# Values of two sets in succession, four buffers of probabilities, and weight rounding in two groups, in a causal attention stage

## The reference

```python
x = x + attn(layernorm(x))            # x: (4, 1024, 256); 16 heads of 16, causal
    q, k, v = proj(x)                 # 256x256 weights and a bias each
    scores = einsum('bhqd,bhkd->bhqk', q, k) / 4 ; future keys masked
    out = softmax(scores) @ v ; out @ wo + bo
x = x + ffn(layernorm(x))             # depth 2: local attention (8 heads of 64, window 128),
                                      # then a gated feed-forward, 256 -> 2*682 -> 256
```

## Time and profile before

| | us |
|---|---|
| median of three runs (2153.69 to 2154.58) | 2154.39 |
| the profiled execution | 2154.2 |
| its span | 2152.4 |
| one group of the causal stage without weight rounding | 31.89 |
| the two groups with it | 39.20 and 40.22 |

### The profile page before, as it was taken

How to read it: one execution, slowest core, us unless ns; L and a number is a source line. 1 busy time by engine, 2 the same in 40 slices (tenths; PEclk the granted TensorE clock), 3 DMA queues, 4 the chain that set the end, 5 groups by cost and what they waited for, 6 DMA issues and landing times.

```text
span 2152.4 us, 36235 instructions
## 1 busy us (share of the span) xinstructions
PE 1969.0 (91%) x12064; PEld 1246.0 (58%) x12064; DVE 1466.1 (68%) x3928; ACT 1261.3 (59%) x3013; POOL 757.0 (35%) x632
## 2 busy tenths in 40 slices
PE   7978999999897669999999999998999999999998
PEld 4522333333234447777677676676777677777766
DVE  7778888888862557568567567557757756856854
ACT  4526666666664337647547646645755764754763
POOL 1033221121322466056146136336515605604610
PEclk9969999999999879999999999999999999999999
DMA  6667534535315620000000000023001000000000
GB/s 181 165 116 149 67 47 61 68 51 97 64 66 146 183 84 1 21 20 1 21 15 6 21 11 11 1 81 113 2 20 40 2 20 30 11 21 20 21 1 30
DMA packets 105447, 112.28 MB, mean 52 GB/s; under 512 B 49801, under 2 KB 84273, under 8 KB 104241
## 3 DMA queue, kind: packets, MB, share of 16 engines
q1 hardware_dynamic: 104688, 101.06, 20.8%
q0 software_dynamic: 576, 8.91, 1.1%
HBM read 67.21 MB, written 42.47 MB: 51 GB/s over the span
## 4 chain that ended last, share of the span: by engine, by line
PE 47%; DVE 6%; ACT 6%; issue 3%; POOL 3%; DVEq 0%; ACTq 0%; POOLq 0%
PE qkv_ps L1370 11%; PE s_ps L1416 5%; PE pt_ps L1487 5%; PE s_ps L1474 4%; PE o_ps L1512 3%; PE qkv_ps L1432 3%; PE pt_ps L1559 3%; POOL inv_norm L1840 2%; PE o_ps L1474 2%; PE pt_ps L1474 2%; PE s_ps L1432 2%; ACT x_all L1685 2%; PE o_ps L1559 2%; PE turn_ps L1396 2%; PE turn_ps L1496 1%
## 5 line engine op out<-in xcount | busy, mean ns | idle before, releaser
L690 ACT ACTIVATE probs<-st_ps 128x512 f32<-128x512 f32 (+3 forms) x768 | 330.0, 495 | 165.5 <-PE st_ps L595 164.9
L1370 PE MATMUL qkv_ps<-w_qkv,x_parts 128*128 128x512 f32 x1152 | 312.6, 416 | 26.6 <-DVE x_all L1932 18.8
L580 PE MATMUL s_ps<-k_stack,q_stack 96*128 96x512 bf16 (+3 forms) x768 | 242.6, 347 | 36.5 <-DVE piece_negmax L735 25.6
L735 DVE CUSTOM_DVE_ANT_0 att_in<-s_ps,causal 128x128 f32<-128x128 f32 (+3 forms) x512 | 233.5, 484 | 42.1 <-PE s_ps L580 42.0
L1370 PEld LDWEIGHTS qkv_ps<-w_qkv,x_parts 128*128 128x128 f32 x1152 | 216.9, 197 | 76.6 <-issue 33.6
L1955 DVE CUSTOM_DVE_ANT_0 x_all<-s_ps,band 128x256 f32<-128x256 f32 (+1 forms) x512 | 178.4, 402 | 112.0 <-PE s_ps L1416 111.3
L1685 ACT ACTIVATE x_all<-x_all,negmax 128x256 f32<-128x256 f32 (+1 forms) x512 | 249.4, 491 | 6.3 <-DVE negmax L1955 5.4
L595 PE MATMUL st_ps<-q_stack,k_stack 98*128 98x512 bf16 (+3 forms) x768 | 241.3, 335 | 12.3 <-ACT probs L690 10.1
L1707 ACT COPY att_in<-pt_ps 128x512 f32<-128x512 f32 (+1 forms) x256 | 143.0, 559 | 149.0 <-PE pt_ps L1487 147.6
L817 POOL TENSOR_SCALAR_AFFINE_SELECT probs<-probs 128x512 f32<-128x512 f32 x128 | 81.4, 636 | 414.6 <-ACT probs L690 414.6
L1848 POOL TENSOR_TENSOR x_all<-x_all,turn_by 128x512 f32<-128x512 f32 x128 | 180.0, 1427 | 101.6 <-PE turn_ps L1396 56.9
(11 more groups left out here) (150 smaller groups left out, 3406.6 us busy)
## 6 DMA issues: line engine op xcount, KB each, us to landing
qk_scratch<-parts SPq DMA_DIRECT2D x64, 192.0 KB, 2.8
q_stack<-qk_scratch SPq DMA_DIRECT2D x96, 128.0 KB, 6.7
k_stack<-qk_scratch SPq DMA_DIRECT2D x96, 128.0 KB, 7.1
w_ffn<-ffn_weights POOLq DMA_DIRECT2D x4, 2176.0 KB, 11.5
x_in<-xt_scratch SPq DMA_DIRECT2D x16, 512.0 KB, 4.2
ffn_weights<-w_high SPq DMA_DIRECT2D x2, 2176.0 KB, 7.7
ffn_weights<-w_raw SPq DMA_DIRECT2D x2, 2176.0 KB, 13.4
att_scratch<-att SPq DMA_DIRECT2D x32, 128.0 KB, 2.0
```

Of the source, the lines that this page charges most:

```text
L580: pe.matmul(s_ps[i % 3][:, 0:kw], q_stack[0:STK, slot, h, qt * P:(qt + 1) * P], k_stack[0:STK, slot, h, k0:k0 + kw], start=True, stop=True ...
L690: act.activation(probs[:, n % 3, h, q0:CH], st_ps[i % 3][:, q0:CH], ACT.Exp).then_inc(exp_done.sem, 1)
L735: dve.tensor_tensor_reduce(seen[:, i % 3, 0:kw], s_ps[i % 3][:, 0:kw], causal[:, CH - kw:CH], -1.0, BIG, ALU.add, ALU.min, result).then_in ...
L1370: mm = pe.matmul(qkv_ps[:, part * CH:(part + 1) * CH], x_parts[:, w % XR, xp, k, :], w_qkv[:, wp, k, part * INNER:(part + 1) * INNER], sta ...
```

## The change

Three edits.

1. PE makes the values only at the end of even sets, two sets in succession: at the end of set n those of n-2 and n-1. Half 0 is turned at the end of set 8 instead of 7, with DVE's `normalise(group, 0)` moved in the same way to step 35.
2. `probs` has four buffers instead of three; ACT waits for the values of set n-4.
3. The weight rounding is done in halves: two copies and two subtractions in each of the groups (0,1), (0,2), (3,1), (3,2); `w_high` is half as wide and each half is stored by itself.

```diff
-        probs = sb("probs", [P, 3, HG, CH])
+        probs = sb("probs", [P, 4, HG, CH])
-        w_high = sb("w_high", [P, WCOLS])
+        w_high = sb("w_high", [P, WCOLS // 2])
...
-            return group in ((0, SPLIT_SLOT), (B - 1, SPLIT_SLOT))
+            r, half = group[0], group[1] - SPLIT_SLOT
+            return (r // (B - 1), half) if r in (0, B - 1) and half in (0, 1) else None
...
                     if i % HG == HG - 1:
-                        if n >= 1:
-                            add_values(group, n - 1)
-                        elif previous:
-                            add_values(previous, NS - 1)
+                        if n % 2 == 0:
+                            for ready in (n - 2, n - 1):
+                                if ready >= 0:
+                                    add_values(group, ready)
+                                elif previous:
+                                    add_values(previous, NS + ready)
...
-                        if n == 7:
+                        if n == 8:
...
                             turn_output(group, 0)
                 if not following:
+                    add_values(group, NS - 2)
                     add_values(group, NS - 1)
...
-                    act.wait_ge(pv_done.sem, when(pv_done, group, NS, n - 3))
+                    act.wait_ge(pv_done.sem, when(pv_done, group, NS, n - 4))
...
-                for i in range(4):
-                    cols = slice(i * PIECE, (i + 1) * PIECE)
-                    act.copy(as_fast(w_high[:, cols]), w_raw[:, cols]).then_inc(w_high_done.sem, 1)
+                for i in range(2):
+                    cols = slice((2 * half + i) * PIECE, (2 * half + i + 1) * PIECE)
+                    act.copy(as_fast(w_high[:, i * PIECE:(i + 1) * PIECE]), w_raw[:, cols]).then_inc(w_high_done.sem, 1)
...
-                    if i == 7 * HG + HG - 1:
+                    if i == 8 * HG + HG - 1:
                         normalise(group, 0)
...
-                        low_parts(group[0] // (B - 1))
+                        low_parts(*splits(group))
```

## The result

| | before | changed |
|---|---|---|
| median, us | 2154.04 | 2199.66 (2194.19 to 2203.12) |
| the profiled execution | 2154.2 | 2199.4 |
| ratio, 95% interval | | 1.0202 (1.019 to 1.0215) |

The account below looks back on a forecast made before the run. PE, though busiest, was taken as coupled to DVE by a ring of three pieces and the join, DVE pacing some stretches. 2154.2 plus 21 (15 groups x 1.4) plus 2 for rounding gave 2177 us, range 2150 to 2190.

Parts of the forecast that it names:

- The walk: PE and DVE followed through each of six stretches of a group in the new order; +1.4 us a group.
- E: Stretch of sets 9 and 10, 4.80 us before: PE idles for the join before `shift_rows`; 5.95 us, +1.15.
- A: Stretch of sets 1 and 2, 5.18 us before: values of set 0 no longer cover PE's wait on ACT's ring; +0.2 us.
- B: Stretch of sets 3 and 4, 3.69 us before: values of set 2 no longer cover `normalise` of half 1; +0.2 us.
- C: Stretch of sets 5 and 6, 7.29 us before, DVE-paced: join of half 0 comes earlier against the start; -0.25 us.
- D: Stretch of sets 7 and 8, 7.08 us before: the 0.19 us saved is eaten by DVE starting empty; +0.05 us.
- F: Stretch of set 11 and set 0 of the next group, 3.85 us before: no change, 0 us.
- the 0.05 for the mask: Sets 9 and 10: POOL's mask of set 9 starts with the join and can hold its cast; +0.05 us, bounds 0 and 0.6.
- Edit 3: Rounding in halves in four groups: 17.6 us over plain groups against 15.6 before, so +2; bounds 8 and 22.
- The join's hold: Rounding groups: POOL's two subtractions delay the join 3.4 to 3.6 us, its cast 2.2; ACT's copies lie beside it.
- rival 1: Whole stage: drains decide, slack takes up moved waits, 18 us go; 2138 us, or 2147 for half; 13%.
- Rival 3: Rounding groups: each of four stalls as long as one did, 31 us instead of 15.6, +15; 2190 us in all; 7%.

Follow-up runs that it names:

- e4: Changed kernel with the last piece before `shift_rows` of half 1 computed ten times, so PE works while it would wait; 2184.48 us, ratio 1.0124 to before.
- e3: Changed kernel with only the values of set 8 put back to the end of set 9, in front of `shift_rows`; 2167.69 us, ratio 1.0056 to before.
- e2: Kernel before with only the weight rounding done in halves in four groups, old order of values, three buffers; 2165.51 us, ratio 1.0038.
- e10: Changed kernel with ACT's two weight copies per rounding group moved from behind step 16 to behind steps 23 and 25; 2175.77 us, ratio 1.0086 to before.
- e1: Kernel before with only the new order of values, turn and normalise, three buffers and the old rounding; 2190.41 us, ratio 1.0148.
- e6: Kernel before with values in succession only for sets 2 and 3, 4 and 5, 10 and 11, rest as before; 2155.93 us, ratio 1.0000.

## Why the prediction was off

**The walk was right.** Its stretches against what the group at full clock measured: E 5.95 and 5.89; A +0.2 and +0.11 (5.29); B +0.2 and +0.15 (3.84); C -0.25 and -0.42 (6.87); D +0.05 and -0.01 (7.07); F 0 and -0.04 (3.81). `shift_rows` was put at 3.29 after E's start and came at 3.28. In all +0.88 a group, where the text took +1.4: the small stretches were taken 0.4 too high together, E 0.06, and the 0.05 for the mask is inside E.

**The step that failed is the price of an idle PE.** "E: +1.15 us" took the microseconds of the wait and nothing for what follows. PE's wait of 1.43 us brought 1.2 GHz for the rest of the stretch, and E measured 7.5. That is about 1.5 us in nine of ten plain groups, 13 us in all, the largest part of the 22 us that the profiled execution took beyond the 2177. The evidence stood in the prediction itself: under edit 3 it read the lower clock off the windows after PE had stood, and priced it there only. `e4` shows this term alone, `e3` that one block is its cause. For 15 groups the order itself came out smaller than forecast, 13 us instead of 21, so the miss would have been larger without that error the other way.

**Edit 3 came out just above its upper bound.** 17.6 us over plain groups were taken, 22 was the bound. In `e2` the four are 4.9, 5.3, 6.3 and 6.0 over (the last against 30.87, the period of that group before), 22.5 in all. The join's hold was right (2.34 us for the cast); ACT's copies were said to lie beside it, but come first. In one of `e2`'s groups:

```profile
582.37 0.39 PE L597 MATMUL st_ps<-q_stack,k_stack 98*128 98x512 bf16 x1 [1.25 <-ACT probs L692]
...
586.33 0.61 PE L582 MATMUL s_ps<-k_stack,q_stack 96*128 96x512 bf16 x1 [2.92 <-DVE piece_negmax L738]
```

That is 4.2 us of standing, the same in all four, where 3.6 were forecast; the 0.7 to 2.1 us that are left go with a clock of 0.91 to 0.95 in these windows. In the changed kernel the two waits are 0.54 and 3.29 us in the group at 606.65. The Trainium skill, "SBUF — State Buffer", section "SBUF: two separate sides", has the lock held for a whole instruction; the cast's 2.34 us beside subtractions of 2.5 (4.96 for two) agrees, and `e10` shows that the place of the subtractions, not their sum, sets the price.

**Edit 2.** "The fourth buffer is what makes edit 1 legal" was wrong: `e1` keeps three. The buffer takes 8.2 KB a partition, and the narrower `w_high` gives 8.7 KB back. Whether both would have fitted at full width, and so whether the buffer is the reason for the halving that costs 8 us, was not tried.

**Rivals.** Pairs of sets can save time, as rival 1 has it: 0.42 us a group for three of them in `e6` (31.89 to 31.47). They did not decide, and whether it is the drains that are saved there or a moved wait is not shown. The period that the prediction names for rival 1, 31.1, does not follow from its own 1.14 us a group, which gives 30.75; both are far from what came. Rival 3 put the rounding at 31 us over plain groups instead of 15.6; alone it came to 22.5, about half of that way.

**The terms now**, between the two profiled executions, 45.3 us apart. The order costs 12 in fourteen groups; the lower clock 13 in the ten plain ones; the rounding by itself 7 (its windows in `e2`; 8 by the ratio). Another 7 are in the four rounding groups, where both edits meet. Their clock is 0.84 to 0.91 against 0.91 to 0.95 in `e2`, about 17 us more at the lower level; at the 1.5 us that 3.4 us of it cost in a plain group this would be some 7.5 us, an estimate. It is not the long wait of stretch E that brings it there, for `e3` lacks that wait and these groups still last 38.0 to 39.7; the cause stays open. The remaining 6 are in the last group (24.2 us against 21.8), 1.1 ahead of the first window, and 2.8 in later stages, whose code did not change and whose time after the last turn lay between 1486.3 and 1490.1 in all runs. These were not tried apart.

## What to carry to other kernels

A block of independent work that stands in front of a wait is worth what it covers of that wait; before grouping such blocks to save a switching cost, walk each wait and ask which block covered it. Price an idle PE twice: the wait, and the products behind it at the lower clock, where the clock falls. When helper work (rounding, stores) is moved, look at what it holds back on each queue it touches: here first the join, then two transfers of 4 KB behind 4 MB.

## What the hardware showed unexpectedly

- The same wait of 1.43 us was followed by the 1.2 GHz level in nine of ten plain groups and not in the tenth. A wait of 0.59 (`e3`), or of 0.45 after filling (`e4`), was never followed by it in plain groups. In `e10` the wait of 1.43 us is in two rounding groups whose whole window has the clock at 1.00. What decides between the two cases is not shown.
- Nine redundant products per group made the kernel 17 us faster (`e4` against the changed kernel).
- A DVE cast of 16 columns takes 0.17 us alone, 0.49 beside a POOL mask and 2.34 beside a POOL subtraction.
